# Selective scan of a four-layer network: operations of 1,024 elements, scans one step ahead, and a reordered opening

## The chip, the cores and the metric

One core of one Trainium2 chip. The metric is the device time of one execution in microseconds; "before" ran three times.

## What is computed

The reference runs four layers on 4,096 tokens of 128 features (fp32); each layer is a feed-forward part, a mixing part and another feed-forward part. The change lies in the mixing part of the last layer, a Mamba block with residual, over 16 sequences of 256 tokens:

```
xz = x @ in_proj_w.T;  xc, z = split(xz)             # 256 channels each
xc = silu(depthwise_conv4(xc) + conv_b)
dt, B, C = split(xc @ x_proj_w.T, [8, 24])           # 8, 16, 16 columns
delta = softplus(dt @ dt_proj_w.T + dt_proj_b)
h[t] = exp(delta * A) * h[t-1] + (delta * xc) * B    # per channel and state, A = -exp(A_log), 16 states
y = sum_over_states(h * C) + xc * D
x = x + (y * silu(z)) @ out_proj_w.T                 # x normalized twice before the block
```

## The kernel before

The whole network is one program of eleven stages; the state x stays in SBUF as 32 tiles of 128 tokens. The stage is the function `mamba` (lines 3635 to 4142). It works on 8 groups of 4 tiles (512 tokens, two sequences). The 256 channels are two halves j of 128 partitions. A group has 16 steps, one for each of the 16 states, so there are 128 steps, n = 16k + s.

**A step.** GpSimd's `inputs(n)` (L3753) multiplies delta*xc by the state's row of B, for each half. ScalarE's `decays(n)` (L3883) writes exp(delta*A) for each half into a PSUM bank. VectorE's `scan(n, j)` (L3974) runs the recurrence along the 512 tokens; a huge step size at a sequence's first token (L3742, L4013) clears the state there. TensorE's `spread_c(n)` (L4086) spreads the state's row of C over the partitions, by a matmul with a selection matrix (`sel`). VectorE's `outputs(n, j)` (L3982) multiplies h by it, and TensorE's `accumulate(n, j)` (L4093) sums that over the states in PSUM with an identity matmul. Inputs, decays, h and products have two buffers for each half: `decays(n)` and `inputs(n)` wait for scan n-2.

**The order** is written out by hand, and each engine's queue runs in order. VectorE: `scan(n, 0)`, `scan(n, 1)`, at s = 0 `gather` of the last group (L3989), `outputs(n, 0)`, `outputs(n, 1)`, at s = 13 the residual add (L3996). TensorE, in pass n: `accumulate(n, 0)`, `spread_c(n+1)`, `accumulate(n, 1)`, then one piece of the next group. ScalarE, in pass n: `decays(n+1)`, then its piece of the next group, which mostly reads what TensorE wrote a pass earlier:

```
for n in range(STEPS):                          # ScalarE, L3911
    k, s = divmod(n, N)
    if n + 1 < STEPS:
        decays(n + 1)
    if k + 1 < GROUPS:
        if s in (1, 2, 3, 4):
            read_xz(k + 1, s - 1)
        if s == 6:
            read_conv(k + 1)
        if s == 8:
            silus(k + 1)
```

TensorE's pieces: `xz` (L4051) at s = 0 to 3, half convolutions (L4063) at s = 4 to 7, `x_proj` (L4070) at 8, `dt` (L4078) at 9 and 10, the last group's output projection (L4103) at 12, transposes (L4042) at 14. They share one bank, `misc`. ScalarE's: `read_xz` (L3826) at 1 to 4, `read_conv` (L3840) at 6, `silus` (L3845 to L3849) at 8, `read_dbc` (L3855) at 9, `read_dt` (L3865, L3866) at 10 and 11, `next_part` (L3859) at 11 and 13, `softplus` (L3871, L3874) at 12, and normalized rows (L3801) and residual tiles (L3812) between. GpSimd's pass n is `inputs(n+1)`, then `split_rows` (L3723 to L3728, which cuts B and C into bf16 parts) at 9 and 11, `step_sizes` (L3733) at 13, `steps_by_inputs` (L3738) and the edge's memsets at 14, `gate_output` (L3759) at 0. SP stores B's rows to HBM and loads them back spread over all partitions (L3713).

**The opening** (L3998 to L4013 and the like on each engine) has no steps to hide under: moments of the first four tiles, their inverse root by Newton steps on GpSimd (`rs[0].pool`, L151 to L164; `dve_newton`, L166, is the same on VectorE), the selection matrix by memset and three selections in fp32 on GpSimd (L3763, L3767) with a copy to bf16 on ScalarE (L3897), the convolution's taps (L3889) after all weights, then projections, convolutions, Silu, step sizes and first inputs of group 0.

Of the kernel before, what the change touches and what calls it, by code (L numbers as in the profile page):

```python
# [3634 lines left out]
def mamba(nc, c, name, w):  # L3635
# [7 lines left out]
    with Phase(nc, name + "m") as ph:  # L3643
# [31 lines left out]
        dA = [[ph.bank(f"dA{j}{i}") for i in range(2)] for j in range(CC)]  # L3675
        yb = [ph.bank(f"y{i}") for i in range(CC)]
        first_xz, first_conv, first_dt = (mb, dA[1][1], *yb), (mb, dA[0][1]), (mb, cbk)

        weights, made, padded, selected, turned_taps, rates, negated = (
            ph.sem(s) for s in ("weights", "made", "padded", "selected", "turned_taps", "rates", "negated"))  # L3680
# [36 lines left out]
        def _(g):  # L3717
# [17 lines left out]
            def steps_by_inputs(k):  # L3735
                for j in range(CC):
                    g.wait_ge(dl_ready, CC * k + j + 1)
                    G.tensor_tensor(du[j][k % 2][:, :], dl[j][k % 2][:, :], xs[j][k % 2][:, :], ALU.mult  # L3738
                                    ).then_inc(du_ready, 1)
                for j in range(CC):  # L3740
                    hold(g, c.mark_g, du_ready, CC * k + j + 1)
                    G.memset(dl[j][k % 2][:, SEQ:SEQ + 1], EDGE).then_inc(edge, 1)  # L3742

            def inputs(n):
                k, s = divmod(n, N)
                if n == 0:
                    g.wait_ge(du_ready, CC)
# [24 lines left out]
            inputs(0)  # L3772
            for n in range(STEPS):
# [3 lines left out]
                if s == 0 and k >= 1:  # L3777
# [517 lines left out]
```

## Time and profile before

| | us |
|---|---|
| three runs | 3350.40, 3343.85, 3349.98; median 3349.98 |
| the profiled execution | 3351.04, its span 3349.30 |
| busy: TensorE, VectorE, GpSimd, ScalarE | 2545.6, 2050.8, 1884.4, 1395.3 |
| this stage | from 2302 to 2832 of the span |
| scans (L3974), 256 | 300.7 busy, 1.214 each |
| products (L3982), 256 | 162.1 busy, 0.677 each |
| inputs (L3753), 256 | 318.0 busy, 1.271 each |
| decays (L3883), 256 | 167.3 busy, 0.682 each |

Times in the trace count from the start of the span. In a timeline a line is: start, duration, engine, line of the kernel, operation, output and inputs, shapes, and how many were merged; two merged operations overlap a little, since one's writing ends after the next has begun. In brackets stands the idle time of the engine before, and what ended it. PE is TensorE, PEld its weight load, DVE VectorE, ACT ScalarE, POOL GpSimd, SPq the queue of SyncE. An fp32 matmul shows as two records.

### The profile page before, as it was taken

The numbers are of one execution on the slowest core, as the hardware profiler recorded it, in microseconds if no ns is written. First come the engines' busy times: TensorE is split into PE (matmuls) and PEld (weight loads), VectorE is DVE, ScalarE is ACT, GpSimd is POOL, SyncE is SP. The second block draws the span as 40 slices with busy tenths as digits, with TensorE's granted clock in tenths as the row PEclk, the third lists the DMA queues.
The fourth block names the chain that finished last, engine by engine and source line by source line (L and its number), as shares of the span: only waits on it lengthen the run. The fifth ranks groups of instructions, "written<-read, shape, count | busy, mean of one in ns | idle before, by whom it ended". The sixth has DMA issues, their size and how long they took to land. (4 is left out here: it accounts for less than half of the span.)

```text
span 3349.3 us, 69215 instructions
## 1 busy us (share of the span) xinstructions
PE 2545.6 (76%) x24495; PEld 1645.0 (49%) x24514; DVE 2050.8 (61%) x6095; ACT 1395.3 (42%) x2956; POOL 1884.4 (56%) x2224
## 2 busy tenths in 40 slices
PE   3438975879994658899978999572887885999772
PEld 2228873556883434555545555460333332555462
DVE  6862225773334545588835787314999999788613
ACT  2202212322221315266642666335666662466433
POOL 4776772574774212299952134573778887124564
PEclk8679996869997879799987999795899998899886
DMA  9207973222996632010001011223121120111133
GB/s 374 80 3 187 221 184 80 74 82 73 227 223 190 221 88 105 14 20 19 14 2 21 20 27 40 67 69 110 51 79 74 51 91 21 19 23 35 46 92 97
DMA packets 222727, 294.18 MB, mean 88 GB/s; under 512 B 36704, under 2 KB 179583, under 8 KB 216288
## 3 DMA queue, kind: packets, MB, share of 16 engines
q1 hardware_dynamic: 168544, 245.65, 23.6%
q0 software_dynamic: 47616, 39.44, 6.3%
q10 hardware_dynamic: 6272, 5.24, 0.6%
q8 instruction: 174, 2.85, 0.4%
q14 instruction: 121, 0.99, 0.1%
HBM read 181.88 MB, written 107.12 MB: 86 GB/s over the span
## 5 line engine op out<-in xcount | busy, mean ns | idle before, releaser
L4093 PE MATMUL l3am_y<-l3am_hc,ident 128*128 128x512 f32 x512 | 284.5, 640 | 78.3 <-DVE l3am_hc L3982 77.2
L3753 POOL TENSOR_TENSOR l3am_db<-l3am_du,l3am_bs 128x512 f32<-128x512 f32 x256 | 318.0, 1271 | 45.6 <-DVE l3am_hh L3974 44.8
L3974 DVE TENSOR_TENSOR_SCAN l3am_hh<-l3am_dA,l3am_db 128x512 f32<-128x512 f32 x256 | 300.7, 1214 | 21.2 <-ACT l3am_dA L3883 11.8
L1200 POOL TENSOR_TENSOR l2a_pT<-l2a_pT,kept 128x512 int32<-128x512 int32 x224 | 278.2, 1280 | 46.0 <-ACT l2a_pT L1406 46.0
L3045 POOL DMA_INDIRECT l0f_table<-l0f2e_y,l0f2e_idx x128 | 178.8, 1397 | 77.9 <-issue 33.6
L3045 POOL DMA_INDIRECT l0f_table<-l0f1e_y,l0f1e_idx x128 | 179.5, 1402 | 68.4 <-issue 32.5
L1287 DVE CUSTOM_DVE_ANT_0 l2a_junk<-l2a_s,addend 128x256 f32<-128x256 f32 x486 | 178.2, 421 | 61.3 <-PE l2a_s L1523 46.7
L1873 POOL DMA_INDIRECT l0f_rows<-l0f1r_row,l0f1r_idx x160 | 163.8, 1024 | 73.2 <-issue 51.1
L4093 PEld LDWEIGHTS l3am_y<-l3am_hc,ident 128*128 128x128 f32 x512 | 96.0, 200 | 205.1 <-DVE l3am_hc L3982 143.7
L3883 ACT ACTIVATE l3am_dA<-l3am_dl,l3am_al 128x512 f32<-128x512 f32 x256 | 167.3, 682 | 58.5 <-POOL l3am_dl L3742 29.7
L1280 DVE TENSOR_REDUCE l3f1a_mx<-l3f1a_s 128x2 f32<-128x512 f32 x243 | 156.4, 685 | 40.4 <-PE l3f1a_s L1523 31.4
L1280 DVE TENSOR_REDUCE l3f2a_mx<-l3f2a_s 128x2 f32<-128x512 f32 x243 | 156.5, 685 | 39.5 <-PE l3f2a_s L1523 31.2
L1546 PE MATMUL l2a_e<-l2a_qk 32*128 32x256 f32 x964 | 162.8, 414 | 11.5 <-DVE l2a_pT L1208 11.2
L1406 ACT ACTIVATE l3f2a_pT<-l3f2a_e 128x512 f32<-128x512 f32 x241 | 133.1, 596 | 80.8 <-PE l3f2a_e L1546 78.3
L1406 ACT ACTIVATE l3f1a_pT<-l3f1a_e 128x512 f32<-128x512 f32 x241 | 133.2, 596 | 79.5 <-PE l3f1a_e L1546 77.0
L3982 DVE TENSOR_TENSOR l3am_hc<-l3am_hh,l3am_c 128x512 f32<-128x512 f32 x256 | 162.1, 677 | 2.8 <-remote 1.6
L1523 PE MATMUL l3f1a_s<-l3f1a_qk 32*128 32x256 f32 x972 | 159.1, 421 | 2.6 <-DMA l3f1a_qk<-l3f1a_none 1.7
L1523 PE MATMUL l2a_s<-l2a_qk 32*128 32x256 f32 x972 | 155.9, 423 | 5.8 <-DMA l2a_qk<-l2a_none 4.2
L1523 PE MATMUL l3f2a_s<-l3f2a_qk 32*128 32x256 f32 x972 | 159.0, 421 | 0.9 <-DVE l3f2a_mx L1280 0.9
L1546 PE MATMUL l3f1a_e<-l3f1a_qk 32*128 32x256 f32 x964 | 152.7, 411 | 0.1
L1546 PE MATMUL l3f2a_e<-l3f2a_qk 32*128 32x256 f32 x964 | 152.6, 411 | 0.1
L1873 POOL DMA_INDIRECT l0f_rows<-l0a_row,l0a_idx x128 | 124.8, 975 | 38.6 <-issue 38.6
(840 smaller groups left out, 6918.3 us busy)
## 6 DMA issues: line engine op xcount, KB each, us to landing
l3am_bs<-l3a_b SPq DMA_DIRECT2D x32, 1024.0 KB, 6.7
l0f1m_w<-in_L_ffn_expert_w SPq DMA_DIRECT2D x64, 384.0 KB
l0f2m_w<-in_L_ffn_expert_w SPq DMA_DIRECT2D x64, 384.0 KB
l0f_rows<-blank SPq DMA_DIRECT2D x8, 1930.0 KB, 22.1
l0f1m_w<-in_L_ffn_expert_w SPq DMA_DIRECT2D x64, 192.0 KB
l0f2m_w<-in_L_ffn_expert_w SPq DMA_DIRECT2D x64, 192.0 KB
l1a_top<-l1a_kernel SPq DMA_DIRECT2D x12, 1024.0 KB, 11.9
l3f_rows<-blank SPq DMA_DIRECT2D x8, 1440.0 KB, 11.8
```

The lines of the kernel that those rows point to most:

```text
L1200: self.nc.gpsimd.tensor_tensor(t, t, self.kept[:, f // 8 % 2, :].unsqueeze(1).to_broadcast([P, 2, 2 * P]), ALU.mult).then_inc(self.cut_g, 1)
L1280: self.nc.vector.tensor_reduce(self.mx[n % 3][:, t, col:col + 2], self.score_bank(f)[:, :].rearrange("p (h s) -> p h s", h=2), AX_X, ALU.m ...
L1287: m = self.nc.vector.tensor_tensor_reduce(out=self.junk[:, 2 * (f % 2) + q, :], in0=self.score_bank(f)[:, 2 * P * q:2 * P * q + 2 * P], in ...
L1406: self.nc.scalar.activation(self.pT[f % self.NP][:, :], self.prob_bank(f)[:, :], ACT.Exp).then_inc(self.p_ready, 1)
L1523: m = self.nc.tensor.matmul(self.score_bank(f)[:, 2 * P * q:2 * P * q + 2 * P], self.qk[n % 4][rows, s, 0, t * P:(t + 1) * P], self.qk[n % ...
L1546: m = self.nc.tensor.matmul(self.prob_bank(f)[:, 2 * P * q:2 * P * q + 2 * P], self.qk[b % 4][rows, s, 1, kh * P:(kh + 1) * P], self.qk[b ...
L1873: g.indirect_dma_start(out=self.m.rows, out_offset=bass.IndirectOffsetOnAxis(ap=self.idx[u][:, t, j:j + 1], axis=0), in_=self.row[u][:, t, ...
L3045: g.indirect_dma_start(out=tables[p], out_offset=bass.IndirectOffsetOnAxis(ap=idx[u % RING][:, a:a + 1], axis=0), in_=y[u % RING][:, a, :] ...
L3753: G.tensor_tensor(db[j][n % 2][:, :], du[j][k % 2][:, :], bs[s // QUARTER][:, s % QUARTER, :], ALU.mult).then_inc(db_ready[j], 1)
L3883: A.activation(dA[j][n % 2][:, :], dl[j][k % 2][:, :], ACT.Exp, scale=al[:, j, s:s + 1]).then_inc(dA_ready, 1)
L3974: V.tensor_tensor_scan(hh[j][n % 2][:, :], dA[j][n % 2][:, :], db[j][n % 2][:, :], 0.0, ALU.mult, ALU.add).then_inc(h_ready, 1)
L4093: T.matmul(yb[j][:, :], c.ident[:, :], hc[j][n % 2][:, :], start=(s == 0), stop=(s == N - 1)).then_inc(summed, 1)
```

## The change

- Inputs, scans and products work on both halves at once, 1,024 elements; `dA` becomes two PSUM tensors of two banks. The second half gets a clearing step size at its start too.
- Inputs have four buffers, h three, decays and products two as before.
- VectorE runs `scan(n + 1)` ahead of `outputs(n)`. TensorE's pass starts with `spread_c(n + 1)`, then both sums of step n. Where the next group's pieces stand in the passes of TensorE and ScalarE stays.
- `silus` ends with the load of a table set that has Exp and Ln. `gate_output` moves from s = 0 to 2, `residual(0)` to step 14.
- The opening: the first root and the first inputs are VectorE's, the Relus, and the bf16 copies of group 0 too; `sel` is made in bf16 directly, after the first scales; the taps' weights are loaded first and waited for alone; tables are loaded early; z's projection comes after `x_proj`, its Silu with those of group 1; `decays(1)` comes before the rows of group 1, and `spread_c(0)` before their transposes.

```diff
+    def pair(self, name):
+        return self.ctx.enter_context(self.nc.psum_tensor(f"{self.name}_{name}", [P, 1024], F32))
...
+        DB, HH = 4, 3
+        db, hh, hc = ([ph.sb(f"{n}{i}", [P, CC * GT]) for i in range(r)] for n, r in (("db", DB), ("hh", HH), ("hc", 2)))
-        dA = [[ph.bank(f"dA{j}{i}") for i in range(2)] for j in range(CC)]
+        dA = [ph.pair(f"dA{i}") for i in range(2)]
...
         def _(sp):
+            sp.dma_start(cw[:], w["L3_attn_conv_w"]).then_inc(taps_in, 16)
...
             def inputs(n):
-                for j in range(CC):
-                    if n >= 2:
-                        g.wait_ge(h_ready, 2 * n - 3 + j)
-                    G.tensor_tensor(db[j][n % 2][:, :], du[j][k % 2][:, :], bs[s // QUARTER][:, s % QUARTER, :], ALU.mult
-                                    ).then_inc(db_ready[j], 1)
+                if n >= DB:
+                    g.wait_ge(h_ready, n - DB + 1)
+                G.tensor_tensor(db[n % DB][:, :].rearrange("p (j t) -> p j t", j=CC), du[k % 2][:, :, :],
+                                bs[s // QUARTER][:, s % QUARTER, :].unsqueeze(1).to_broadcast([P, CC, GT]), ALU.mult
+                                ).then_inc(db_ready, 1)
...
-            rs[0].pool(g, 0)
+            g.wait_ge(scaled, 3)
+            G.memset(sel[:, :, :], 0.0).then_inc(made, 1)
...
             def silus(k):
+                if k == 1:
+                    a.wait_ge(z_read, CC)
+                    for j in range(CC):
+                        A.activation(zs[j][0][:, :], zs[j][0][:, :], ACT.Silu).then_inc(silu_z, 1)
...
+                A.preload_act_table_set("natural_log_exp_and_others")
...
             def decays(n):
+                if n >= 2:
+                    a.wait_ge(h_ready, n - 1)
                 for j in range(CC):
-                    if n >= 2:
-                        a.wait_ge(h_ready, 2 * n - 3 + j)
-                    A.activation(dA[j][n % 2][:, :], dl[j][k % 2][:, :], ACT.Exp, scale=al[:, j, s:s + 1]
+                    A.activation(dA[n % 2][:, halves[j]], dl[j][k % 2][:, :], ACT.Exp, scale=al[:, j, s:s + 1]
                                  ).then_inc(dA_ready, 1)
...
+            A.preload_act_table(ACT.Silu)
+            a.wait_ge(taps_in, 16)
...
             rs[part].dve(v, var[part][:, :, :].rearrange("p i t -> p (i t)"), 0, 1.0, 0.0)
+                if part == 0:
+                    rs[0].dve_newton(v)
...
+            V.tensor_tensor(db[0][:, :].rearrange("p (j t) -> p j t", j=CC), du[0][:, :, :],
+                            bs[0][:, 0, :].unsqueeze(1).to_broadcast([P, CC, GT]), ALU.mult).then_inc(first_db, 1)
+            scan(0)
             for n in range(STEPS):
-                for j in range(CC):
-                    scan(n, j)
+                if n + 1 < STEPS:
+                    scan(n + 1)
                 if s == 0 and k >= 1:
                     gather(k - 1)
-                for j in range(CC):
-                    outputs(n, j)
+                outputs(n)
...
             def spread_c(n):
                 if n:
-                    pe.wait_ge(hc_ready, CC * n)
+                    pe.wait_ge(hc_ready, n)
...
             for n in range(STEPS):
-                accumulate(n, 0)
                 if n + 1 < STEPS:
                     spread_c(n + 1)
-                accumulate(n, 1)
+                for j in range(CC):
+                    accumulate(n, j)
```

## Rows read from the trace of the kernel before

**Rows 1.** Stretches: length, busy PE, PEld, DVE, ACT, POOL (operations), clock, DMA, GB/s.

```profile
2302.00:2343.00 41.00, 16.97 (x36) 7.17 (x36) 17.47 (x88) 22.15 (x36) 18.49 (x35) 0.67 0.32 117
...
2405.00:2465.00 60.00, 51.00 (x132) 21.79 (x132) 57.27 (x67) 40.94 (x67) 50.09 (x45) 0.97 0.19 71
```

**Rows 2.** Timeline of VectorE, steps of groups 0, 1 and 7.

```profile
2343.73 2.34 DVE L3974 TENSOR_TENSOR_SCAN l3am_hh<-l3am_dA,l3am_db 128x512 f32<-128x512 f32 x2 [2.10 <-ACT l3am_dA L3883]
...
2356.97 2.33 DVE L3974 TENSOR_TENSOR_SCAN l3am_hh<-l3am_dA,l3am_db 128x512 f32<-128x512 f32 x2
2359.22 1.26 DVE L3982 TENSOR_TENSOR l3am_hc<-l3am_hh,l3am_c 128x512 f32<-128x512 f32 x2
...
2363.82 2.33 DVE L3974 TENSOR_TENSOR_SCAN l3am_hh<-l3am_dA,l3am_db 128x512 f32<-128x512 f32 x2
...
2407.50 1.38 DVE L3989 SCALAR_TENSOR_TENSOR l3am_yT<-l3am_xs,l3am_dd,l3am_y 128x512 f32<-128x512 f32 x2
...
2467.39 1.38 DVE L3989 SCALAR_TENSOR_TENSOR l3am_yT<-l3am_xs,l3am_dd,l3am_y 128x512 f32<-128x512 f32 x2
...
2821.63 1.26 DVE L3982 TENSOR_TENSOR l3am_hc<-l3am_hh,l3am_c 128x512 f32<-128x512 f32 x2
```

**Rows 3.** Timeline of TensorE, group 0, and the start of group 2.

```profile
2359.94 1.12 PE L4093 MATMUL l3am_y<-l3am_hc,ident 128*128 128x512 f32 x2 [0.37 <-DVE l3am_hc L3982]
...
2361.98 1.02 PE L4051 MATMUL l3am_misc<-l3am_xnT,l3am_win 128*128 128x512 f32 x2
...
2376.35 1.88 PE L4063 MATMUL l3am_misc<-l3am_xpad,l3am_taps 128*128 128x512 f32 x4
...
2469.42 2.07 PE L4093 MATMUL l3am_y<-l3am_hc,ident 128*128 128x512 f32 x2 [3.96 <-DVE l3am_hc L3982]
```

**Rows 4.** Timeline of ScalarE, group 0.

```profile
2359.61 0.60 ACT L3826 ACTIVATE l3am_zs<-l3am_misc 128x512 f32<-128x512 f32 x1 [0.96 <-PE l3am_misc L4051]
...
2360.49 1.29 ACT L3883 ACTIVATE l3am_dA<-l3am_dl,l3am_al 128x512 f32<-128x512 f32 x2
...
2378.27 0.69 ACT L3849 ACTIVATE l3am_xs<-l3am_misc,l3am_cb 128x512 f32<-128x512 f32 x1 [0.83 <-PE l3am_misc L4063]
2378.97 1.28 ACT L3883 ACT_TABLE_LOAD   x1
...
2388.08 0.69 ACT L3865 ACTIVATE l3am_ra<-l3am_misc,l3am_dtb 128x512 f32<-128x512 f32 x1 [0.72 <-PE l3am_misc L4078]
...
2389.37 0.63 ACT L3859 ACTIVATE l3am_parts<-l3am_rest 64x512 bf16<-64x512 f32 x1
```

**Rows 5.** Timeline of GpSimd, groups 0 and 1.

```profile
2382.68 0.61 POOL L3723 CAST l3am_parts<-l3am_dbc 128x512 bf16<-128x512 f32 x1 [4.78 <-ACT l3am_dbc L3855]
...
2384.48 4.95 POOL L3753 TENSOR_TENSOR l3am_db<-l3am_du,l3am_bs 128x512 f32<-128x512 f32 x4
...
2411.13 9.87 POOL L3753 TENSOR_TENSOR l3am_db<-l3am_du,l3am_bs 128x512 f32<-128x512 f32 x8
```

**Rows 6.** Groups by line, VectorE: count | busy us, mean ns | idle before.

```profile
L1715 DVE TENSOR_TENSOR l0f1r_big<-l0f1r_big 128x1024 f32<-128x1024 f32 x15 | 18.4, 1224 | 0.4
...
L3184 DVE TENSOR_TENSOR l3f_src<-l3f_src,l3f1c_nw 128x512 f32<-128x512 f32 x8 | 5.5, 690 | 8.1 <-ACT l3f_src L3166 8.1
...
L174 DVE TENSOR_TENSOR l0f1r_rln_t<-l0f1r_rln_y 128x4 f32<-128x4 f32 x24 | 3.9, 164 | 0.8
```

**Rows 7.** Timeline of the opening, ScalarE, then VectorE.

```profile
2309.25 2.45 ACT L3889 ACTIVATE l3am_taps<-ident,l3am_cw 128x128 f32<-128x128 f32 x8 [9.16 <-DMA l3am_wo<-in_L_attn_out_proj_w]
2311.60 1.64 ACT L3801 ACTIVATE l3am_xn<-x_state,l3am_shift,l3am_ln_y 128x128 f32<-128x128 f32 x4
...
2309.35 1.94 DVE L3963 SCALAR_TENSOR_TENSOR l3am_shift<-l3am_mv,l3am_ln_y 128x4 f32<-128x4 f32 x1 [3.75 <-POOL l3am_ln_y L164]
```

**Rows 8.** DMA issues on the page: count, size, us to landing.

```profile
l3am_bs<-l3a_b SPq DMA_DIRECT2D x32, 1024.0 KB, 6.7
```

**Rows 9.** A stretch of TensorE: length, busy, clock, DMA, GB/s.

```profile
2470.00:2472.50 2.50, 2.50 (x4) 0.50 0.00 0
```

More of the change, by code:

```diff
@@ L3674, in mamba @@
         mb, cbk = ph.bank("misc"), ph.bank("c")
[L3675 removed]
+        dA = [ph.pair(f"dA{i}") for i in range(2)]
         yb = [ph.bank(f"y{i}") for i in range(CC)]
[L3677 to L3680 removed]
+        halves = [slice(j * GT, (j + 1) * GT) for j in range(CC)]
+        first_xz, first_conv, first_dt = (mb[:, :], dA[1][:, halves[1]], yb[0][:, :], yb[1][:, :]), (
+            mb[:, :], dA[1][:, halves[0]]), (mb[:, :], cbk[:, :])
+        weights, taps_in, made, padded, turned_taps, rates, negated, relued, first_db, z_read = (
+            ph.sem(s) for s in ("weights", "taps_in", "made", "padded", "turned_taps", "rates", "negated", "relued", "first_db",
+                                "z_read"))
+        WEIGHTS = 160
         stats, moments, variances, scaled, rows_ready, turned, xnT_ready, x_ready = (
@@ L3776, in _ @@
                     inputs(n + 1)
-                if s == 0 and k >= 1:
+                if s == 2 and k >= 1:
                     gate_output(k - 1)
@@ L3891, in _ @@
             rows(0)
+            a.wait_ge(weights, WEIGHTS)
             turned_rows(0)
@@ L3895, in _ @@
                 read_xz(0, j)
-            a.wait_ge(made, 4)
-            A.activation(sel[:, :, :], self_[:, :, :], ACT.Copy).then_inc(selected, 1)
             first_silus()
+            A.preload_act_table_set("natural_log_exp_and_others")
+            A.activation(al[:, :, :], al[:, :, :], ACT.Exp).then_inc(rates, 1)
             read_dbc(0)
+            first_z(0)
             read_dt(0, 0)
             read_dt(0, 1)
-            A.activation(al[:, :, :], al[:, :, :], ACT.Exp).then_inc(rates, 1)
             softplus(0)
-            next_part(0, 1)
-            next_part(0, 2)
             a.wait_ge(negated, 1)
             decays(0)
+            decays(1)
+            first_z(1)
             rows(1)
             turned_rows(1)
-            residual(0)
             for n in range(STEPS):
                 k, s = divmod(n, N)
-                if n + 1 < STEPS:
+                if 1 <= n < STEPS - 1:
                     decays(n + 1)
+                if n == 14:
+                    residual(0)
                 if k + 1 < GROUPS:
@@ L4049, in xz @@
                     pe.wait_ge(xz_read, 4 * k + j - CC)
-                bank = mb if k else first_xz[j]
-                T.matmul(bank[:, :], win[:, j * P:(j + 1) * P], xnT[k % 2][:, :], start=True, stop=True
+                bank = mb[:, :] if k else first_xz[j]
+                T.matmul(bank, win[:, j * P:(j + 1) * P], xnT[k % 2][:, :], start=True, stop=True
                          ).then_inc(xz_done, 1)
@@ L4076, in dt @@
                     pe.wait_ge(dt_read, CC * k + 1)
-                bank = mb if k else first_dt[j]
-                T.matmul(bank[:, :], dtw[:, j * P:(j + 1) * P], dbc[0:RK, :], start=True, stop=True).then_inc(dt_done, 1)
+                bank = mb[:, :] if k else first_dt[j]
+                T.matmul(bank, dtw[:, j * P:(j + 1) * P], dbc[0:RK, :], start=True, stop=True).then_inc(dt_done, 1)
             def spread_c(n):
@@ L4105, in output @@
                 m.then_inc(o_done, 1)
-            pe.wait_ge(weights, 176)
             turn(0)
+            pe.wait_ge(weights, WEIGHTS)
             for j in range(CC):
```

113 lines of the change are left out of this document (64 added, 49 removed).

## The prediction

> **What bounds the kernel now.** I read the stretches first [rows 1]: the change lies in one stage, the selective scan, an opening of 41 us (2302 to 2343) and then 128 steps to 2822.9. In 60 us, a group, VectorE is busy 57.3, TensorE 51.0, GpSimd 50.1, ScalarE 40.9. So VectorE bounds the steps, and the others have room on average. Its timeline shows how [rows 2]: a step is two scans and two products, and the starts at 2356.97 and 2363.82 are two steps of 3.43. Then I followed who waits for whom inside a step, in the timelines of TensorE, ScalarE and GpSimd [rows 3 to 5]. The projections of the next group ride along: TensorE computes one, ScalarE reads it, and as ScalarE's queue is in order, the decays of a later step stand behind that read. Now this costs nothing. In the step from 2356.97 TensorE begins with the first product at 2359.94 and the xz matmul ends at 2363.00 [rows 3]. The read of the step before, at 2359.61, lets the decays finish at 2361.78 [rows 4], for a scan that starts at 2363.82: 2 us of slack.
>
> **The steps, price by price.** Two scans take 2.25 us (2356.97 to 2359.22), so two products 1.18 of the 3.43. A product of 1,024 lasts 0.534 longer than one of 512 (1.224 and 0.690 [rows 6]), so of the pitch of 0.59 some 0.056 belongs to the instruction. No row has a scan of another length; I give it the same 0.056. One scan of 1,024 comes to 2.19 (ready after 2.28), one product to 1.12 (1.21): a step of 3.31, 14 us less over 128 steps. Bounds: 3.20 if the scan's own part is three times as large, 3.43 if an operand over two banks costs as two operations. I take 3.31, nearest to the rows. The Trainium skill (Perfetto Trace Analysis, the part on optimization) gives some 60 ns per VectorE instruction on SBUF and 125 on PSUM, and says that larger operations help a saturated engine. By its PSUM figure this term would be 32 us, an estimate; the trace has 0.056.
> GpSimd's product goes from 1.23 each (9.87 for 8 [rows 5]) to one of 2.35; bounds 2.1 and 2.5.
>
> **The order moves too, and this decides.** VectorE now runs scan(n+1), then outputs(n). TensorE's extra work of step n waits for outputs(n), hence for scan(n+1). ScalarE still reads it in its pass n+1, ahead of decays(n+3), and with two decay buffers it can't have run further ahead. This chain spanned three steps before (2356.97 to 2363.00, and 2.2 on ScalarE: 8.2 us used of 10.3); now it has two, 6.6 us. Let T(n) be the start of scan(n) in a group.
> Leg A, xz (four in a group): scan 2.19, product 1.21, spread, sums and xz 3.06 plus 0.04 [rows 3], read, rows and decays 2.17 (2359.61 to 2361.78 [rows 4]), handing over 0.05: T(n+2) is at least T(n)+8.72. T1 to T3 is 10.15, as the gather pair (1.38 [rows 2]) lies between, T3 to T5 8.72, T5 to T6 3.31: 22.2.
> Leg B, read of convolution 0: TensorE, still busy with the half before, gets to the second at T6+3.9, sums 1.94, half a convolution 1.88 [rows 3], read and decays 1.9 [rows 4]: T6 to T8 9.65, not 6.62.
> Leg C: T8, outputs(7) 3.40, sums and half a convolution 3.96, Silu 0.69: T8+8.1. Behind it on ScalarE stands the table load that the change puts there, 1.28, then decays(10), 1.29: T10 is T8+10.6. x_proj (1.88), after the sums of pass 8, ends at T8+11.0, its copy 0.6; GpSimd's split, behind which inputs(11) stands, takes 1.80 (2382.68 to 2384.48 [rows 5]), the input 2.35: T8 to T11 15.85, not 9.93. Four input buffers don't help, since GpSimd itself stands at the split.
> Leg D: T11, outputs(10) 3.40, sums and dt 3.1, Relu and Abs 1.29, part 0.65 [rows 4], rest 1.15, input 2.35: T13 is T11+11.95, not 6.62.
> Leg E, GpSimd alone: inputs 14, 15, 16 (7.0), two sizes and two products at 1.23 (4.9), memsets 0.3: T13 to T16 12.2, against 9.93 plus the residual add, 0.7. T16 to T17 3.31.
> Sum: 75.2 us a group, where it was 59.9 (the gathers at 2407.50 and 2467.39 [rows 2]). Total: first step 2.2, group 0 without gather 73.8, six groups 451.2, the last group, with no extra work, 47.7, its add 0.7, last scan and two products 4.5: 580.1. Before: first scan at 2343.73 to the last product's end, 2822.89, 479.2 [rows 2]. **+100.9.**
> At leg C a rule speaks on the load's price. The row has ScalarE start it 0.01 after the Silu and end after 1.28 [rows 4]. The Trainium skill (ScalarE: Activation LUTs, What ACT_TABLE_LOAD costs) adds a drain, 2.66 us for a switch; by it T10 would come 1.4 later, 9 us in seven groups by an estimate. The row doesn't bear the drain out.
> Costed at nothing: two table loads a group around Ln go, 2.6 us of ScalarE, but GpSimd, still at inputs 13 and 14, is late next. residual(0) moves to step 14, where ScalarE has little due; gate_output to step 2, where GpSimd has room. Without that cover, 1.6 once and 2.5 a group. SP's reloads wait for one input fewer: covered by three other quarters.
>
> **The opening.** VectorE waited 3.75 for the root from GpSimd, and its next operation took 1.94 for 128x4 [rows 7], alongside a selection. The root on VectorE costs nine operations of 0.2 (3.9 plus 0.8 idle for 24 [rows 6]), 1.8, and selections and memset come later. With the taps loaded first (in the kernel before they wait for all weights until 2309.25), rows(0) starts near 2306.9, not 2311.60 [rows 7], and the weights just don't hold xnT: -4.7. z's matmuls leave the front of x_proj, and the rates go under it: -1.2. Two Relus (-1.3) and the table loads before Exp, Ln and the first decays (1.28 each, -3.9) leave ScalarE's path. The selection's copy lay under the convolutions: 0. Against it stand the first inputs on VectorE, 1,024 long, 1.2 to 1.7 where the pair on GpSimd overlapped, less 0.8 in that rows and products are interleaved: about +0.9. Scan 0 moves from 2343.73 to near 2333.5: **-10.2**. Bounds: -13, if nothing waits, and -5, if B's rows of 1 MB, 6.7 us from issue to landing [rows 8], come after the step sizes.
>
> **TensorE's clock.** At the group's edge TensorE idled 3.96 before 2469.42 [rows 3], and the granted clock was then 0.50, the 1.2 GHz level [rows 9]. In my schedule it idles 5.9 us before outputs(12). Five us at that level put 2.5 on the output projection, for which VectorE's add waits: T16 comes 2.1 later in six groups, **+12.6**. Bounds: 0, and 126, all 18 us of TensorE work on the legs of seven groups at half speed.
> Sum: 100.9 - 10.2 + 12.6 = +103.3. The profiled execution took 3351.04 (span 3349.30), 1.06 above the median of the runs, 3349.98: so 3453.3 against the median.
>
> **Rivals.** (1) *VectorE stays the bound*, and the waits are hidden as now. 128 steps of 3.31 with seven gathers and adds are 437 where it was 479.2; with -10.2 that gives 3298, faster. For it: VectorE's 57.3 of 60 [rows 1], more buffers for inputs and states. Against: the decays keep two, and ScalarE's read sits where it sat. It decides at one place: whether ScalarE's read of xz begins at least 2.2 us before the scan behind it is due. Chance 0.12.
> (2) *Only ScalarE's chains cost*, and GpSimd's inputs 11, 13 and 16 come in time: the stops of 20.3 us a group become about 14.6, in seven groups 40 less: 3413. 0.13.
> (3) *The clock falls through most of a group*: half the upper bound, some 3510 to 3520. For it: 0.67 in the opening [rows 1]. 0.10.
> (4) *The wide operations gain nothing* (two banks cost as two operations): 14 more on a path that mostly waits, near 3457. 0.05.
> (5) Stops of a third of mine cancel the gains: no change. 0.02.
> My forecast has 0.58.
>
> **The numbers.** 3453. The range leaves out (1), (5) and (3): from (2) with 13 for the clock off, 3400, to the forecast with 47 more for clock and legs, 3500. A measurement of this kernel tells about 0.2%, 7 us, from no change. Faster 0.12, same 0.02, slower 0.86.
>
> **What would show it.** Right: scans of 1,024 near 2.28 us and products near 1.21; VectorE idle some 20 us a group, before scans 3, 5, 8, 10 and 12 for ScalarE's decays and before 11, 13 and 16 for GpSimd's inputs; gathers 75 us apart; the last group at 3.3 a step; scan 0 about 10 us earlier. Wrong: VectorE idle below 3 us a group and gathers 55 apart (rival 1).

## The result, and the profile after

The changed kernel takes 3512.85 us (median of four runs, 3507.07 to 3513.38), the kernel before 3349.37 on the same chip (3343.85 to 3350.4): a ratio of 1.0486, 95% interval 1.0471 to 1.0501, 163.5 us slower. Slower was forecast, by 103, within a range that ended at 3500.

| | before | forecast | after |
|---|---|---|---|
| the profiled execution, its span | 3351.04, 3349.30 | | 3513.21, 3511.5 |
| opening, first operation of the stage to scan 0 | 41.39 | 31.2 | 32.84 |
| scan 0 to the end of the last product | 479.2 | 580.1 + 12.6 | 648.3 |
| a group (gather to gather) | 59.9 | 75.2, 77.3 with the clock | 85.3 |
| the last group | | 52.9 | 52.0 |
| ScalarE's table loads in the stage, each | 1.28 | 1.28 | 1.28 |

The span grew by 162.2; the stage by 169.1 - 8.6 = 160.5. So nearly the whole difference lies in the stage. Against the forecast at full clock, group 0 took 10.0 more (86.0 to its gather, 76.0 forecast) and the next six 59.1 (510.3 and 451.2); the last one, which has no next group to prepare, runs as forecast.

First the groups by line. The scan's row carries the result: its own time fell from 300.7 to 292.5, its waiting is 185.3.

```profile
L3762 POOL TENSOR_TENSOR l3am_db<-l3am_du,l3am_bs 128x1024 f32<-128x1024 f32 x127 | 297.3, 2361 | 65.1 <-DVE l3am_hh L4001 61.4 <-DVE l3am_du L4045 3.5
L4001 DVE TENSOR_TENSOR_SCAN l3am_hh<-l3am_dA,l3am_db 128x1024 f32<-128x1024 f32 x128 | 292.5, 2286 | 185.3 <-ACT l3am_dA L3901 130.6 <-issue 54.6
L4009 DVE TENSOR_TENSOR l3am_hc<-l3am_hh,l3am_c 128x1024 f32<-128x1024 f32 x128 | 153.2, 1197 | 2.6 <-PE l3am_c L4125 2.1 <-issue 0.5
```

Then VectorE's timeline in group 1, which answers to [rows 2]. Steps without a stop are 3.31 apart (2430.67 to 2433.99). Stops stand before steps 3, 5, 8 and 10 (ScalarE's decays) and before 11 (GpSimd's input, shown as "issue": that input ends as the scan starts). Behind them come 3.29 before step 12 and 4.38 before 13 (in groups 2 to 5 it is 0.42 and 6.67), and 3.02 before 17.

```profile
2417.12 2.28 DVE L4001 TENSOR_TENSOR_SCAN l3am_hh<-l3am_dA,l3am_db 128x1024 f32<-128x1024 f32 x1
2421.18 1.41 DVE L4018 SCALAR_TENSOR_TENSOR l3am_yT<-l3am_xs,l3am_dd,l3am_y 128x512 f32<-128x512 f32 x2 [1.77 <-PE l3am_y L4132]
...
2430.67 2.29 DVE L4001 TENSOR_TENSOR_SCAN l3am_hh<-l3am_dA,l3am_db 128x1024 f32<-128x1024 f32 x1 [3.64 <-ACT l3am_dA L3901]
...
2433.99 2.28 DVE L4001 TENSOR_TENSOR_SCAN l3am_hh<-l3am_dA,l3am_db 128x1024 f32<-128x1024 f32 x1
...
2441.03 2.29 DVE L4001 TENSOR_TENSOR_SCAN l3am_hh<-l3am_dA,l3am_db 128x1024 f32<-128x1024 f32 x1 [3.65 <-ACT l3am_dA L3901]
...
2455.60 2.29 DVE L4001 TENSOR_TENSOR_SCAN l3am_hh<-l3am_dA,l3am_db 128x1024 f32<-128x1024 f32 x1 [4.07 <-ACT l3am_dA L3901]
...
2466.25 2.29 DVE L4001 TENSOR_TENSOR_SCAN l3am_hh<-l3am_dA,l3am_db 128x1024 f32<-128x1024 f32 x1 [3.94 <-ACT l3am_dA L3901]
...
2471.57 2.29 DVE L4001 TENSOR_TENSOR_SCAN l3am_hh<-l3am_dA,l3am_db 128x1024 f32<-128x1024 f32 x1 [1.92 <-issue]
...
2486.04 2.29 DVE L4001 TENSOR_TENSOR_SCAN l3am_hh<-l3am_dA,l3am_db 128x1024 f32<-128x1024 f32 x1 [4.38 <-issue]
```

The stops stand where the forecast put them, but are longer. TensorE's timeline says why; it answers to [rows 3].

```profile
2434.13 0.39 PE L4125 MATMUL l3am_c<-l3am_parts,l3am_sel 128*128 128x512 bf16 x1 [2.91 <-DVE l3am_hc L4009]
2434.35 3.37 PE L4132 MATMUL l3am_y<-l3am_hc,ident 128*128 128x512 f32 x4
2437.51 1.27 PE L4090 MATMUL l3am_misc<-l3am_xnT,l3am_win 128*128 128x512 f32 x2
2438.62 0.38 PE L4125 MATMUL l3am_c<-l3am_parts,l3am_sel 128*128 128x512 bf16 x1
2438.84 1.88 PE L4132 MATMUL l3am_y<-l3am_hc,ident 128*128 128x512 f32 x4
```

TensorE idles 2.91 us, and then the four sums take 3.37 where the next four take 1.88. The stretches show the granted clock (the number before the last two of each line): 0.82 over group 1, where group 1 of the kernel before had 0.97 [rows 1], 0.62 in the first 2.5 us of that step, 0.50 at 2470, and 1.00 in the last group, in which VectorE is busy 52.47 of 54.

```profile
2421.00:2506.00 85.00, 62.99 (x133) 25.75 (x132) 54.34 (x35) 37.23 (x62) 47.62 (x27) 0.82 0.13 50
2434.00:2436.50 2.50, 2.37 (x4) 1.07 (x5) 2.50 (x3) 0.00 (x0) 1.48 (x2) 0.62 0.00 0
2470.00:2472.50 2.50, 2.50 (x4) 1.03 (x4) 0.93 (x1) 0.00 (x0) 2.50 (x2) 0.50 0.89 364
2929.00:2983.00 54.00, 34.73 (x96) 14.54 (x96) 52.47 (x34) 17.05 (x27) 33.15 (x16) 1.00 0.00 0
```

The legs of group 3, start of scan to start of scan, against the forecast, and two runs told below (T(n) is the start of scan n of the group). They sum to the gathers' distance:

| leg | forecast | after | TensorE kept busy | busier still |
|---|---|---|---|---|
| A, T1 to T6 | 22.2 | 25.02 | 21.95 | 21.96 |
| B, T6 to T8 | 9.65 | 11.12 | 9.56 | 9.56 |
| C, T8 to T11 | 15.85 | 15.97 | 15.98 | 16.83 |
| D, T11 to T13 | 11.95 | 13.89 | 13.78 | 12.21 |
| E, T13 to T16 | 12.2 | 12.90 | 12.80 | 13.00 |
| T16 to T17 | 3.31 | 6.41 | 4.72 | 4.72 |
| group | 75.2 | 85.3 | 78.8 | 78.3 |

### The profile page after: what moved, and what is told of

Same layout as the page of the kernel before. It is cut to its first block and busy times, and to the rows that moved or that the text cites. A ratio compares the mean times of both kernels' runs of the same rounds, so it can differ in the third digit from the quotient of the medians.

```text
span 3511.5 us, 68571 instructions
## 1 busy us (share of the span) xinstructions
PE 2598.4 (74%) x24514; PEld 1666.7 (47%) x24514; DVE 2043.8 (58%) x5853; ACT 1369.0 (39%) x2937; POOL 1864.1 (53%) x2083
## 5 line engine op out<-in xcount | busy, mean ns | idle before, releaser
L4001 DVE TENSOR_TENSOR_SCAN l3am_hh<-l3am_dA,l3am_db 128x1024 f32<-128x1024 f32 x128 | 292.5, 2286 | 185.3 <-ACT l3am_dA L3901 130.6
L3762 POOL TENSOR_TENSOR l3am_db<-l3am_du,l3am_bs 128x1024 f32<-128x1024 f32 x127 | 297.3, 2361 | 65.1 <-DVE l3am_hh L4001 61.4
L4132 PE MATMUL l3am_y<-l3am_hc,ident 128*128 128x512 f32 x512 | 308.0, 736 | 0.0
L1876 POOL DMA_INDIRECT l0f_rows<-l0f1r_row,l0f1r_idx x160 | 163.8, 1024 | 73.2 <-issue 51.1
L4125 PE MATMUL l3am_c<-l3am_parts,l3am_sel 128*128 128x512 bf16 x128 | 56.5, 442 | 197.0 <-DVE l3am_hc L4009 194.3
L3901 ACT ACTIVATE l3am_dA<-l3am_dl,l3am_al 128x512 f32<-128x512 f32 x256 | 165.5, 680 | 78.8 <-POOL l3am_dl L3752 41.0
L1283 DVE TENSOR_REDUCE l3f2a_mx<-l3f2a_s 128x2 f32<-128x512 f32 x243 | 156.3, 684 | 39.3 <-PE l3f2a_s L1526 31.2
L4132 PEld LDWEIGHTS l3am_y<-l3am_hc,ident 128*128 128x128 f32 x512 | 119.7, 234 | 102.5 <-issue 96.7
L4009 DVE TENSOR_TENSOR l3am_hc<-l3am_hh,l3am_c 128x1024 f32<-128x1024 f32 x128 | 153.2, 1197 | 2.6 <-PE l3am_c L4125 2.1
```

Of the source, the lines that this page charges most:

```text
L1283: self.nc.vector.tensor_reduce(self.mx[n % 3][:, t, col:col + 2], self.score_bank(f)[:, :].rearrange("p (h s) -> p h s", h=2), AX_X, ALU.m ...
L1876: g.indirect_dma_start(out=self.m.rows, out_offset=bass.IndirectOffsetOnAxis(ap=self.idx[u][:, t, j:j + 1], axis=0), in_=self.row[u][:, t, ...
L3762: G.tensor_tensor(db[n % DB][:, :].rearrange("p (j t) -> p j t", j=CC), du[k % 2][:, :, :], bs[s // QUARTER][:, s % QUARTER, :].unsqueeze( ...
L3901: A.activation(dA[n % 2][:, halves[j]], dl[j][k % 2][:, :], ACT.Exp, scale=al[:, j, s:s + 1]).then_inc(dA_ready, 1)
L4001: V.tensor_tensor_scan(hh[n % HH][:, :], dA[n % 2][:, :], db[n % DB][:, :], 0.0, ALU.mult, ALU.add).then_inc(h_ready, 1)
L4132: T.matmul(yb[j][:, :], c.ident[:, :], hc[n % 2][:, halves[j]], start=(s == 0), stop=(s == N - 1)).then_inc(summed, 1)
```

## The experiments

Twelve kernels ran, on four chips. Three of the chips take some 3670 to 3690 us for the kernel before (longer stages ahead of this one), so each ratio is to the kernel before on the same chip, and durations are compared inside the stage alone.

**The order alone.** The kernel before, halves of 512 and its own opening, with only VectorE's scans one step ahead (and three h buffers for that):

```diff
+            for j in range(CC):
+                scan(0, j)
             for n in range(STEPS):
-                for j in range(CC):
-                    scan(n, j)
+                if n + 1 < STEPS:
+                    for j in range(CC):
+                        scan(n + 1, j)
```

> The kernel before, with halves of 512 and its old opening, and only VectorE's order changed: both scans of n + 1 ahead of both products of n (three h buffers for each half). If the order is the cause, the same chains appear, each about 1.2 us shorter as halves are handed on earlier: stops of 1 to 3 us at the same steps, 3430 to 3480 us. If the width is the cause, it takes 3345 to 3355 us as before.

Measured: 3786.22 us, ratio 1.0296 [1.0271, 1.0321]; 583 us from scan 0 to the last product where it was 479, and 74.7 from gather to gather (2771.58 to 2846.31). The ratio is inside what was expected. The larger stops stand where the changed kernel has them, before steps 8, 10, 11 and 13:

```profile
2799.84 2.34 DVE L3975 TENSOR_TENSOR_SCAN l3am_hh<-l3am_dA,l3am_db 128x512 f32<-128x512 f32 x2 [1.29 <-ACT l3am_dA L3884]
...
2809.49 2.34 DVE L3975 TENSOR_TENSOR_SCAN l3am_hh<-l3am_dA,l3am_db 128x512 f32<-128x512 f32 x2 [2.72 <-ACT l3am_dA L3884]
...
2826.80 2.44 DVE L3975 TENSOR_TENSOR_SCAN l3am_hh<-l3am_dA,l3am_db 128x512 f32<-128x512 f32 x2 [5.43 <-issue]
```

So the order costs some 100 us by itself, with no wide operation in the kernel. That is not all of the changed kernel's 169: the xz legs, which stop it by some 3.6 before steps 3 and 5, stop this one by 0.2 to 0.5 a step, as each half is handed on alone, and its clock is 0.91 over that group where the changed kernel has 0.82. The other 66 us come from the order and the wide operations together; the next run has the wide operations without the order.

**The order turned back.** The changed kernel, with scan(n) ahead of outputs(n):

```diff
-            scan(0)
             for n in range(STEPS):
                 k, s = divmod(n, N)
-                if n + 1 < STEPS:
-                    scan(n + 1)
+                scan(n)
```

> The changed kernel with VectorE's order of before: scan(n), then outputs(n). Everything else of the change stays. If the order is the cause, TensorE's pieces again come a scan earlier, the chain through ScalarE spans three steps, VectorE is the bound: some 3.4 us a step (the product now follows its own scan at once), groups of 57 us, 3315 to 3335 us. If the width of the operations or the buffers are the cause, it stays near 3513.

Measured: 3685.45, ratio 1.0003 [0.9983, 1.0023]; gathers 61.4 apart where 57 was expected, and the scans wait 24.1 us in all; from scan 0 to the last product 486 us, where the kernel before has 479. The long stops are gone, as expected; the gain is not there. Two reasons stand in VectorE's timeline. A product that follows its own scan starts 2.32 after it, the next scan 1.14 later, so a step is 3.46, not 3.31:

```profile
2697.78 2.28 DVE L4001 TENSOR_TENSOR_SCAN l3am_hh<-l3am_dA,l3am_db 128x1024 f32<-128x1024 f32 x1
2700.10 1.22 DVE L4009 TENSOR_TENSOR l3am_hc<-l3am_hh,l3am_c 128x1024 f32<-128x1024 f32 x1
2701.24 2.28 DVE L4001 TENSOR_TENSOR_SCAN l3am_hh<-l3am_dA,l3am_db 128x1024 f32<-128x1024 f32 x1
```

In the kernel before a step had 3.43, its two halves filling each other's gap. And GpSimd's inputs, now 2.35 whole instead of two of 1.23, come late before steps 11 (1.8 us) and 16 (0.5 to 1.5); the Silu pass adds 0.9 before step 10. The wide operations without the new order are worth nothing here; most of the opening's gain goes back into the steps.

**Pieces first.** The changed kernel, TensorE's piece of the next group ahead of the spread and the sums of the same pass, so that it no longer waits for outputs(n):

```diff
-                if n + 1 < STEPS:
-                    spread_c(n + 1)
-                for j in range(CC):
-                    accumulate(n, j)
                 if k + 1 < GROUPS:
...
+                if n + 1 < STEPS:
+                    spread_c(n + 1)
+                for j in range(CC):
+                    accumulate(n, j)
```

> The changed kernel, scans a step ahead as it has them, but in each TensorE pass the piece of the next group is issued before spread_c(n + 1) and the sums, so it no longer waits for outputs(n). If the wait of the pieces for outputs(n) is the cause, and not running ahead as such, the stops of 3 to 4 us before scans 3, 5, 8, 13 go, groups take 55 to 58 us, and it runs in 3300 to 3325 us. If running ahead itself costs (decay buffers, GpSimd), it stays above 3400.

Measured: 3680.79, ratio 0.9978 [0.9956, 0.9999]; gathers 60.7 and 62.2 apart in turn where they were 85.3, the clock over a group 0.97. The order of four lines on TensorE gives back what the order on VectorE cost: the stops of legs A and B are gone (seven steps of 3.31 in a row). It misses what was expected (groups of 55 to 58), as the stops before steps 10, 11 and 16 (1.6, 1.9, 1.6) remain:

```profile
2731.98 2.29 DVE L4001 TENSOR_TENSOR_SCAN l3am_hh<-l3am_dA,l3am_db 128x1024 f32<-128x1024 f32 x1 [1.64 <-ACT l3am_dA L3901]
2734.19 1.20 DVE L4009 TENSOR_TENSOR l3am_hc<-l3am_hh,l3am_c 128x1024 f32<-128x1024 f32 x1
2737.31 2.29 DVE L4001 TENSOR_TENSOR_SCAN l3am_hh<-l3am_dA,l3am_db 128x1024 f32<-128x1024 f32 x1 [1.93 <-ACT l3am_dA L3901]
```

The second names ScalarE, but the decays were done at 2734.08, and the scan started as GpSimd's input ended: the split of B and C stands ahead of that input.

```profile
2733.06 0.61 POOL L3733 CAST l3am_parts<-l3am_dbc 128x512 bf16<-128x512 f32 x1 [11.32 <-ACT l3am_dbc L3870]
2733.75 1.16 POOL L3735 TENSOR_TENSOR l3am_rest<-l3am_dbc,l3am_parts 128x512 f32<-128x512 f32 x1
2734.87 4.66 POOL L3762 TENSOR_TENSOR l3am_db<-l3am_du,l3am_bs 128x1024 f32<-128x1024 f32 x2
```

GpSimd waited 11.32 us for the split's data while scans 7 to 9 (the last ended at 2729.2) freed three of its four input buffers.

**TensorE kept busy.** The changed kernel with bf16 matmuls by zero where TensorE idles, numbers of them by pass; they add nothing to the sums.

```diff
+        FILL = {1: 10, 3: 10, 8: 11, 11: 16, 13: 7, 15: 16}
...
+                    for i in range(FILL[s]):
+                        T.matmul(bank[:, :], sel[:, 0, :], zero[:, :], start=(s == 15), stop=(s == 15))
```

> The changed kernel with bf16 matmuls of zeros added where TensorE idles longest (10 after passes 1 and 3, 11 after pass 8, 16 after pass 11, 7 after pass 13, 16 after pass 15 of a group), which add nothing to the sums. If the half-speed clock after idle time is what my sum missed, the granted clock stays near 1.00 in the steps, T3 to T5 falls from 10.3 to 8.7 us and a group from 85.3 to about 77: 3445 to 3465 us, in spite of more work. If the missing time is something else, it stays at 3513 or gets longer by the added matmuls.

Measured: 3799.59, ratio 1.0318 [1.0299, 1.0337], inside what was expected; gathers 77.1 to 78.8 apart, 78.1 on the mean where the changed kernel has 85.0. More work on TensorE took 44.4 us off the stage (603.9 from scan 0 to the last product, 648.3 in the changed kernel). The idle before the same pass is 0.75 instead of 2.91, the sums take 1.88, and the group's clock is 0.96 where it was 0.82. The last five rows are the pass of step 10 in group 1, then in group 2:

```profile
2737.97 0.39 PE L4128 MATMUL l3am_c<-l3am_parts,l3am_sel 128*128 128x512 bf16 x1 [0.75 <-DVE l3am_hc L4012]
2738.20 1.88 PE L4135 MATMUL l3am_y<-l3am_hc,ident 128*128 128x512 f32 x4
...
2775.49 0.39 PE L4128 MATMUL l3am_c<-l3am_parts,l3am_sel 128*128 128x512 bf16 x1 [2.17 <-DVE l3am_hc L4012]
2775.72 2.59 PE L4135 MATMUL l3am_y<-l3am_hc,ident 128*128 128x512 f32 x4
2778.24 2.07 PE L4120 MATMUL l3am_misc<-l3am_dbc,l3am_dtw 8*128 8x512 f32 x2
...
2853.14 0.39 PE L4128 MATMUL l3am_c<-l3am_parts,l3am_sel 128*128 128x512 bf16 x1 [2.17 <-DVE l3am_hc L4012]
2853.37 1.88 PE L4135 MATMUL l3am_y<-l3am_hc,ident 128*128 128x512 f32 x4
```

T3 to T5 is 8.66 there, where the forecast had 8.72 and the changed kernel 10.2 to 10.4. Leg D is another matter: no filler stood ahead of pass 10, its sums and the dt matmul behind them ran slow in group 1, and the leg took 13.87, as in the changed kernel. In group 2 the same pass comes after the same idle, 2.17, its sums take 1.88, and the leg took 12.21. So the speed of these matmuls, and not the wait ahead of them, makes the leg's excess; and an idle of this length is followed now by the one speed, now by the other.

**The changed kernel again**, to have it on this chip.

> The changed kernel itself, on this chip, so that the other runs can be set against it: ratio to the kernel before 1.047 to 1.050, gathers 85.3 us apart, scan 0 32.8 us after the stage's first VectorE operation.

Measured: 3839.66, ratio 1.0465 [1.0429, 1.0501], just under what was expected, 648.5 from scan 0 to the last product, and scan 0 33.1 us after the stage's first operation (32.8 on the first chip). By the ratios the run with TensorE kept busy is 1.5% below it.

**Busier.** The same fillers and 4 more after pass 7, 9 after pass 9 (`FILL = {..., 7: 4, ..., 9: 9, ...}`).

> As the run that keeps TensorE busy, with zero matmuls also after passes 7 (4) and 9 (9), so that no idle stands before the sums of pass 10. Mine: the granted clock is 1.00 in the 20 us before the output projection too, step 13 comes 12.0 to 12.4 after step 11 where it was 13.9, and the gathers are 75.5 to 77 us apart (78.1 with fewer fillers, 85.3 without; 75.2 was forecast). Rival (leg D's excess is GpSimd's or ScalarE's, not the clock's): step 13 at 13.5 or more after step 11, gathers at 78.

Measured, one execution: leg D is 12.21 in every group, inside what was expected, so its excess too was the clock's. The stage is 47.7 us shorter than the changed kernel's (600.6 from scan 0). The gathers hardly came closer, 78.3: a miss. The fillers after pass 7 put off x_proj, and leg C grew by 0.86; before pass 12 TensorE still idles 3.34, and its sums took 3.32 and held up the output projection. Fillers are a probe, not a remedy.

**A longer lead.** The changed kernel, with decays two steps ahead instead of one and inputs three ahead. The third decay buffer is in SBUF, as PSUM has no bank left.

```diff
+        AB = 3
-        dA = [ph.pair(f"dA{i}") for i in range(2)]
+        dA = [ph.pair("dA0"), ph.pair("dA1"), ph.sb("dA2", [P, CC * GT])]
...
-                if 1 <= n < STEPS - 1:
-                    decays(n + 1)
+                if n + AB - 1 < STEPS:
+                    decays(n + AB - 1)
...
-                if n + 1 < STEPS:
-                    inputs(n + 1)
+                if k + 1 < GROUPS and s == 13:
+                    step_sizes(k + 1)
+                    steps_by_inputs(k + 1)
+                if n + DB - 1 < STEPS:
+                    inputs(n + DB - 1)
```

> Changed kernel (VectorE's order scan(n+1), outputs(n) kept, TensorE's and ScalarE's pieces in the same passes), but ScalarE computes decays two steps ahead instead of one (a third decay buffer, this one in SBUF, the other two stay in PSUM) and GpSimd computes inputs three ahead instead of one, with step sizes and their products before the first input that needs them. Mine: the stops are the lead's. With a step more of lead the chain TensorE, ScalarE, decays has three steps (9.93 us) for its 8.72, so T1 to T6 and T6 to T8 run at 3.31 a step; only the Silu pass (10.6 for three steps) still shows, some 1 us. Gathers 57 to 60 us apart, scans idle under 4 us a group, ratio to the kernel before 0.978 to 0.990. Rival (ScalarE's and TensorE's queues are too full, or TensorE at half speed, whatever the lead): gathers over 70 apart, ratio over 1.015. Rival (the third buffer in SBUF slows its scans or decays while GpSimd runs): every third scan over 2.5 us, ratio 0.995 to 1.01.

Measured: 3706.13, ratio 1.0088 [1.0061, 1.0115], gathers 63.9 to 66.9 apart, where 0.978 to 0.990 and 57 to 60 were expected. The scans wait 17.4 us in all where they waited 185.4: the stops were the lead's, of both engines together. The rival of the slow third buffer holds too, ratio included: the scans are 339.1 us busy instead of 292.5. The gathers and the residual adds wait another 17.1 for TensorE.

```profile
L4003 DVE TENSOR_TENSOR_SCAN l3am_hh<-l3am_dA,l3am_db 128x1024 f32<-128x1024 f32 x128 | 339.1, 2650 | 17.4 <-ACT l3am_dA L3903 12.9 <-issue 4.2
L3763 POOL TENSOR_TENSOR l3am_db<-l3am_du,l3am_bs 128x1024 f32<-128x1024 f32 x127 | 328.6, 2612 | 36.8 <-DVE l3am_hh L4003 33.1 <-DVE l3am_du L4047 3.5
```

**The longer lead with pieces first**, both edits.

> As the run with the longer lead, and TensorE's piece of the next group goes ahead of the spread and the sums of step n (as in the run with pieces first). Mine: nothing is left that VectorE waits for but the hand-over of GpSimd at steps 13 to 16: gathers 55.3 to 57.5 us apart (16 steps of 3.31, gather pair 1.3, residual add 0.6), stage 440 to 460 from scan 0 to the last product, 8.5 earlier at the start, ratio 0.978 to 0.986. Rival (TensorE is the next bound: its 51 us a group at full speed, with stretches at half speed): gathers 58 to 60, ratio 0.987 to 0.995.

Measured: 3673.22, ratio 1.0009 [0.9990, 1.0028]: outside mine and the rival's. The scans wait 6.3 us in all, so mine was right about their waits, but they are 331.9 busy: the third buffer's 39 us ate the gain, and gathers and adds wait 10.8 for TensorE.

**GpSimd's lead alone**, in the changed kernel: the last part of the edit above, decays as they were.

> Changed kernel with only GpSimd's order changed: inputs three ahead, step sizes and their products ahead of the first input that needs them; VectorE, ScalarE and TensorE as in the changed kernel. Mine: only GpSimd's share of the legs goes (step 11 comes 3.3 after step 10, steps 13 to 16 run without GpSimd's wait), ScalarE's chains with the sums at half speed stay: gathers 76 to 80 us apart where they were 85.3, ratio 1.028 to 1.038. Rival (GpSimd's queue is what sets the group): gathers under 70, ratio under 1.01. Rival (ScalarE's chain stands right behind GpSimd's everywhere): gathers over 83, ratio over 1.042.

Measured: 3465.31, ratio 1.0358 [1.0341, 1.0375], gathers 76.6 to 80.3 apart, as expected. "Issue" is gone from the scan's row, and 147.3 of ScalarE's decays stay. So GpSimd's hand-over is worth about 7 us of a group's 25 over the kernel before (part of it the clock's: T3 to T5 is 8.66 in two of the groups), and the chain over TensorE and ScalarE has most of the rest.

**Pieces first and GpSimd's lead**, decays in their two PSUM pairs.

> As the run with pieces first, and GpSimd runs its inputs three ahead instead of one (the four buffers are there already), with step sizes and their products ahead of the first input that needs them. Decays stay two buffers in PSUM. Mine: the stops before steps 11, 13 and 16 of a group go (2.0, 0.25 and 1.6 us there), the one of 1.7 before step 10 (ScalarE's Silu pass) stays: gathers 56.5 to 58 us apart where they were 60.7, scans 2.28 us each, 27 us less in all, ratio to the kernel before 0.987 to 0.993. Rival (another wait takes their place, TensorE's sums or the edge for the decays): gathers over 59.5, ratio 0.995 to 0.999. Rival (more of GpSimd beside VectorE slows its operations): scans over 2.35 on the mean.

Measured: 3316.24 (3311.79 to 3319.54), where the kernel before took 3345.95 on the same chip: ratio 0.9911 [0.9894, 0.9928]. It beats both kernels, the kernel before by 0.9%, as expected. From gather to gather it is 56.90 six times, the clock is 1.00, and the one stop left is the Silu pass's before step 10.

```profile
L4002 DVE TENSOR_TENSOR_SCAN l3am_hh<-l3am_dA,l3am_db 128x1024 f32<-128x1024 f32 x128 | 291.9, 2281 | 13.1 <-ACT l3am_dA L3902 13.0
```

```profile
2450.80:2507.70 56.90, 48.70 (x131) 21.18 (x132) 55.18 (x36) 38.21 (x63) 47.68 (x28) 1.00 0.19 75
```

**The same with the order turned back**, scan(n), outputs(n), and TensorE's pass as in the changed kernel, sums first.

> As the run with GpSimd's inputs three ahead, but with VectorE's order scan(n), outputs(n) and TensorE's spread and sums ahead of its piece, as in the run in which only VectorE's order was turned back. Mine: the product stands behind its own scan, so a step is 3.455 where it is 3.31, and the rest of the stops is the Silu pass's 1.0: gathers 58 to 59.5 us apart (56.9 with scans one ahead and pieces first, 61.4 with GpSimd one ahead), ratio to the kernel before 0.992 to 0.998. Rival (the order is worth nothing once GpSimd leads): gathers 56.5 to 57.5, ratio 0.990 to 0.992. Rival (without pieces first, ScalarE's reads stop the scans as in the changed kernel): gathers over 62.

Measured: 3654.95, ratio 0.9959 [0.9926, 0.9993], gathers 58.9 to 59.5 apart, a step of 3.46, as expected. So the scan one step ahead, with pieces first, is worth some 2 us a group. The two edits changed together here; the step's 3.46 against 3.31 makes 2.4 of it by an estimate.

**The root back on GpSimd**, in the changed kernel:

```diff
-                if part == 0:
-                    rs[0].dve_newton(v)
...
+            rs[0].pool(g, 0)
             g.wait_ge(scaled, 3)
```

> Changed kernel, with the first inverse root back on GpSimd (its selection memset behind it, as the scales wait for the root). Mine: the root on VectorE is worth what GpSimd's took more, 3.75 of waiting against some 1.8, so scan 0 comes 34.6 to 35.0 us after the stage's first VectorE operation, where it is 32.8 in the changed kernel and 41.4 in the kernel before; nothing later moves. Rival (rows(0) waits for the weights or taps anyway): scan 0 stays at 32.8 to 33.2. Rival (what cost before was the scales' 1.94 alongside a selection, not the engine): under 33.8.

Measured, one execution: scan 0 at 34.3 after the stage's first operation, 33.1 in the changed kernel on this chip, 32.8 before that: 1.2 to 1.5 us for the root, a little under what was expected. VectorE waits 3.77 for it, but the scales then take 0.16, as the selections now come after them:

```profile
2605.56 0.16 DVE L3985 SCALAR_TENSOR_TENSOR l3am_shift<-l3am_mv,l3am_ln_y 128x4 f32<-128x4 f32 x1 [3.77 <-POOL l3am_ln_y L167]
```

## Why the forecast went wrong where it did

**The direction and its cause: right.** The order decides, by the chain VectorE, TensorE, ScalarE. The run with the order alone (+103 in the stage) and the run with pieces first (back to 61.4 a group on the mean) show it from both sides; the wide operations alone cost 7 from scan 0 on, together with the order another 59. The place at which rival 1 was to decide fell against it. The stops stand before steps 3, 5, 8, 10, 11, 12 and 13 as listed (the one before 12 is only 0.42 in groups 2 to 5). From group 1 on there is none before 16: the residual add ahead of scan 15 waits some 2.2 for the output projection, and meanwhile GpSimd catches up, so that leg E took 12.90 where 12.2 and 2.1 for the clock had been summed.

**The step's price: right.** 3.31 forecast, 3.31 measured; scan 2.28, product 1.20. The 0.056 for an instruction held. The Trainium skill (Perfetto Trace Analysis, Optimizing Scalar/DVE Operations) gives 125 ns on PSUM; the trace doesn't agree with that figure.

**TensorE's clock: the step that failed.** The forecast costed one place, T16, from the idle before 2469.42 [rows 3], gave it 12.6, and left the other legs at full speed without a reason. But the legs themselves make idle: while VectorE waits for ScalarE, no product comes, and TensorE waits 2.63, 2.91, 2.90 and 3.18 before the slow passes of legs A to D in group 1. The half speed then lies on the very leg that made the idle, 1.5 from T3 to T5 and 1.5 in leg B: a loop that the sum, worked out at full speed, had left out. The forecast's own leg A held the idle: two passes of 3.06 in 8.72 leave 2.6. The two runs with fillers price it. They took 44.4 and 47.7 us off the stage, and the second lost 0.86 in leg C of seven groups to its own fillers, so the clock has some 54 (an estimate from these two numbers, and a low one, as slow sums are left in pass 12), where 12.6 stood.

Rival 3, which got 0.10, was nearest: the clock falls in many passes of a group, though not through most of it (0.82 over group 1). That its 3510 to 3520 holds the result is in part luck. Half the bound of 126 in place of 12.6 makes 3504 and not 3510 to 3520, and the clock had some 54 of the 126, less than half; other terms fill the difference.

**T16 to T17: forecast 3.31, measured 6.41.** ScalarE turns the rows of two groups ahead in pass 15, behind TensorE's transposes of pass 14, and decays(17) stands behind it. The forecast hadn't followed that read. In groups 2 to 5 of both runs with fillers the sums ahead of these transposes run at full speed, and it is still 4.72: 1.7 of the 3.1 was the clock again, 1.4 is the read's place.

```profile
2588.57 0.78 ACT L3815 ACTIVATE l3am_xnT<-l3am_misc,l3am_lnb,l3am_lnw 128x512 f32<-128x512 f32 x1 [5.76 <-PE l3am_misc L4081]
2589.24 1.29 ACT L3901 ACTIVATE l3am_dA<-l3am_dl,l3am_al 128x512 f32<-128x512 f32 x2
```

**The opening: -8.55, forecast -10.2.** rows(0) starts at 2306.71 (2306.9 forecast), 4.9 earlier. But dbc is read only 4.8 earlier (2324.44 and 2329.27), where the forecast had 5.9: the first convolution took 4.12 instead of 3.60, at a granted clock of 0.87, and x_proj waits 0.78 for the second Silu, a wait that z's matmuls had covered. By the end of Ln (2329.98 and 2338.54) the gain is 8.6. The last 0.4 of the forecast is missing because VectorE, which now copies the second bf16 part, waits 1.27 for GpSimd's rest, and the first step size stands behind that copy, 0.9 after Ln. The copy had been costed at nothing.

```profile
2328.84 1.14 ACT L3890 ACTIVATE l3am_ve<-l3am_ve 128x512 f32<-128x512 f32 x2
...
2330.40 0.42 DVE L4038 CAST l3am_parts<-l3am_rest 32x512 bf16<-32x512 f32 x1 [1.27 <-POOL l3am_rest L3738]
2330.86 0.69 DVE L4042 TENSOR_TENSOR l3am_dl<-l3am_ra,l3am_ve 128x512 f32<-128x512 f32 x1
```

**The table load: right.** It takes 1.28, and the decays start 0.01 after it:

```profile
2549.42 1.28 ACT L3864 ACT_TABLE_LOAD   x1
2550.71 1.30 ACT L3901 ACTIVATE l3am_dA<-l3am_dl,l3am_al 128x512 f32<-128x512 f32 x2
```

T10 is T8 + 10.66 where 10.6 was forecast; with the drain of the Trainium skill (ScalarE: Activation LUTs, What ACT_TABLE_LOAD costs) it would have been 12.0. No run here shows the drain.

Summed against the forecast of +103.3 in the stage: clock 54 in place of 12.6, opening 1.65 less, and some 14 more, which gives the measured 160.5. Of the 14, 4.7 lie in group 0 and 2.1 to 2.7 in each of the next five groups (1.4 of it before step 17, most of the rest in leg E), less 1.6 at the end. What of leg E is clock and what GpSimd's hand-over was not taken apart, nor was group 0.

## What to carry to other kernels

Before an operation is moved ahead of another in a queue, write down for each engine behind it which buffers give it how many steps of lead, and sum the chain around: here a chain of 8.7 us fitted three steps of 3.4 and not two. A stop of the pacing engine also idles TensorE, so work out a leg's TensorE part at the lower clock as well. And give the free buffers to the order: once GpSimd's queue ran three inputs ahead in the four buffers that were there, a group went from 85.0 to 78.0 us, and with pieces first from 61.4 to 56.9.

## What the runs showed of the chip

A scan that reads the decays from PSUM and the inputs from SBUF takes 2.28 to 2.29 whatever GpSimd does (the longest in the run with the longer lead is 2.29). With both in SBUF (every third scan of the run with the longer lead) it took 2.28 to 4.50, 3.41 on the mean, and 2.28 again after GpSimd's last input (at 3131.84). GpSimd's own inputs went from 2.36 to 2.61 on the mean.

```profile
2703.40 4.00 DVE L4003 TENSOR_TENSOR_SCAN l3am_hh<-l3am_dA,l3am_db 128x1024 f32<-128x1024 f32 x1 [0.17 <-ACT l3am_dA L3903]
...
2708.44 2.28 DVE L4003 TENSOR_TENSOR_SCAN l3am_hh<-l3am_dA,l3am_db 128x1024 f32<-128x1024 f32 x1
...
3131.84 2.28 DVE L4003 TENSOR_TENSOR_SCAN l3am_hh<-l3am_dA,l3am_db 128x1024 f32<-128x1024 f32 x1
```

The Trainium skill (SBUF — State Buffer, Who interferes with whom) states this for a VectorE instruction with two SBUF inputs beside a GpSimd instruction that reads SBUF; the trace agrees, with up to 2.2 us on one scan.

Matmuls of no use made a stage shorter by 44 to 48 us: with the idle before a pass cut from 2.91 to 0.75, four sums took 1.88 instead of 3.37. How long an idle has to be was not measured.
